# A four-layer gated cross-attention block: three transfers, a bias and half of the key pieces change engines

## What is computed

```python
x = x + tanh(g_xattn[0]) * L0_attention(layernorm(x), ctx)        # 16 heads of 16
x = x + tanh(g_ffn[0])   * L0_quantised_linear(layernorm(x))      # Hadamard, 4-bit levels, ternary weights
x = x + tanh(g_xattn[1]) * L1_attention(layernorm(x), ctx, mask)  # 16 heads, rotary positions
x = x + tanh(g_ffn[1])   * L1_top1_experts(layernorm(x))
x = x + tanh(g_xattn[2]) * L2_attention(layernorm(x), ctx, mask)  # 16 heads
x = x + tanh(g_ffn[2])   * L2_experts_with_capacity(layernorm(x))
x = x + tanh(g_xattn[3]) * L3_attention(layernorm(x), ctx)        # one head of 256
x = x + tanh(g_ffn[3])   * L3_top2_gated_experts(layernorm(x))
return x
```

```python
q, k, v = heads(x @ Wq + bq), heads(ctx @ Wk + bk), heads(ctx @ Wv + bv)   # 16 heads of 16
a = softmax(q @ k.T * scale, axis=-1)                                      # 512 x 1601 per head
out = concat(a @ v) @ Wo + bo
```

## Time and profile before

| | |
|---|---|
| median of 3 runs | 3863.64 us (3862.93 to 3868.33) |
| the profiled execution: its time | 3879.41 us |
| its span, first to last instruction | 3878.2 us |
| mean granted TensorE clock | 0.936 |
| busy share of the span: PE, DVE, ACT, POOL | 88%, 56%, 52%, 17% |

### The profile page before, as it was taken

The page is one execution under the profiler, slowest core; times in us unless marked ns, Lnnn a source line. Parts: engine busy times, 40 slices in busy tenths (PEclk is TensorE's granted clock), DMA queues, the critical chain, the costliest instruction groups (busy, mean ns, idle before and its releaser), DMA issues.

```text
span 3878.2 us, 52368 instructions
## 1 busy us (share of the span) xinstructions
PE 3417.0 (88%) x18396; PEld 1779.4 (46%) x18396; DVE 2178.5 (56%) x3567; ACT 2034.2 (52%) x4490; POOL 654.5 (17%) x700
## 2 busy tenths in 40 slices
PE   5899999978588899997899799889986979987997
PEld 2333333325332223332588333223325956677996
DVE  6767676736767677873401477768843032265333
ACT  2566666663236566766333267567671322244664
POOL 2111111001224331000302131210002110022331
PEclk8999999999789999999799799999997989998998
DMA  8132323106654443310965665754208521042555
GB/s 191 43 102 63 102 63 102 24 22 194 166 180 113 99 101 74 60 24 13 280 215 168 180 159 117 169 117 98 80 9 279 175 89 68 1 141 89 179 184 171
DMA packets 314686, 456.02 MB, mean 118 GB/s; under 512 B 66315, under 2 KB 234195, under 8 KB 312251
## 3 DMA queue, kind: packets, MB, share of 16 engines
q1 hardware_dynamic: 243382, 292.39, 28.0%
q0 software_dynamic: 29568, 104.65, 8.1%
q10 hardware_dynamic: 41477, 55.63, 5.5%
HBM read 292.46 MB, written 153.91 MB: 115 GB/s over the span
## 4 chain that ended last, share of the span: by engine, by line
PE 65%; DVE 13%; DMA 6%; issue 5%; POOL 4%; ACT 3%; SPq 2%; another core or an unknown queue 0%; ACTq 0%; POOLq 0%; DVEq 0%
PE pv L1334 14%; PE m L1298 10%; DVE mxp L1181 10%; PE s L1320 9%; PE h L2796 5%; PE y L2804 5%; PE h L2370 4%; PE y L2379 3%; PE y L1779 2%; PE s L1759 2%; PE s L1265 2%; PE m L1342 1%; ACT e_t L1412 1%; PE s L1282 1%; DMA ot<-sums 1%
## 5 line engine op out<-in xcount | busy, mean ns | idle before, releaser
L1181 DVE TENSOR_REDUCE mxp<-m 128x1 f32<-128x802 f32 x1536 | 1447.7, 985 | 523.0 <-PE m L1298 519.3
L1412 ACT ACTIVATE e_t<-s 128x512 f32<-128x512 f32 (+1 forms) x2496 | 1339.3, 599 | 575.7 <-PE s L1320 574.8
L1298 PE MATMUL m<-kaug,qaug 97*128 97x401 bf16 x3072 | 813.4, 347 | 115.9 <-DVE mxp L1181 66.3
L1320 PE MATMUL s<-qaug,kaug 100*128 100x512 bf16 (+1 forms) x2496 | 858.8, 387 | 22.6 <-ACT e_t L1412 18.3
L1334 PE MATMUL pv<-e_t,v 128*32 128x512 f32 (+1 forms) x4992 | 672.0, 611 | 0.2
L1320 PEld LDWEIGHTS s<-qaug,kaug 100*128 100x128 bf16 (+1 forms) x2496 | 228.5, 100 | 717.9 <-ACT e_t L1412 495.6
L1298 PEld LDWEIGHTS m<-kaug,qaug 97*128 97x128 bf16 x3072 | 274.1, 100 | 526.9 <-DVE mxp L1181 283.7
L127 POOL TENSOR_TENSOR rstd<-rstd,mhalf 128x16 f32<-128x16 f32 (+2 forms) x9 | 24.2, 2688 | 1207.3 <-DVE rstd L120 1207.3
L2866 ACT ACTIVATE ez<-h,b 128x128 f32<-128x128 f32 x440 | 120.1, 388 | 160.8 <-PE h L2796 160.8
L1334 PEld LDWEIGHTS pv<-e_t,v 128*32 128x32 f32 (+1 forms) x4992 | 98.7, 108 | 214.9 <-ACT e_t L1412 157.2
L2257 DVE SCALAR_TENSOR_TENSOR y<-y,b 128x256 f32<-128x256 f32 x39 | 16.5, 424 | 304.8 <-PE y L2379 304.8
(11 more groups left out here) (370 smaller groups left out, 3559.1 us busy)
## 6 DMA issues: line engine op xcount, KB each, us to landing
w<-in_L_w POOLq DMA_DIRECT2D x78, 1024.0 KB, 5.4
w<-in_L_w SPq DMA_DIRECT2D x24, 1024.0 KB, 12.3
xregion<-zero ACTq DMA_DIRECT2D x10, 2056.0 KB, 13.9
kaug<-kparts SPq DMA_DIRECT2D x16, 1200.8 KB
kaug<-kready SPq DMA_DIRECT2D x32, 600.4 KB
kaug<-kready SPq DMA_DIRECT2D x16, 1200.8 KB
vn<-values SPq DMA_DIRECT2D x8, 1536.0 KB
values<-p_vb ACTq DMA_DIRECT2D x21, 512.0 KB
```

Source lines behind the costliest of these rows:

```text
L1181: dve.tensor_reduce(a.mxp[:, u.g % 2, half, n:n + 1], a.m_slot[u.m % 2][:].rearrange("p (a n) -> p a n", a=2)[:, :, 0:PIECE + 1], AX.XY, A ...
L1298: m = pe.matmul(slot[:, 512 * k:512 * k + PIECE + 1], a.qaug[0:R_MAX, u.g, j, P * qc:P * qc + P], a.kaug[0:R_MAX, u.g, j, k0:k0 + PIECE + ...
L1320: pe.matmul(slot[0:KW[u.k], :], a.kaug[0:R_ALL, u.g, u.j, P * u.k:P * u.k + KW[u.k]], a.qaug[0:R_ALL, u.g, u.j, :], start=True, stop=True) ...
L1412: act.activation(a.e_t[0:KW[u.k], e % 2, u.j, :], a.s_slot[u.s % 3][0:KW[u.k], :], ACT.Exp).then_inc(s_free.sem, 1)
```

## The change

Three things are moved.

1. The store of the reciprocals and their spreading go from SP's queue to ACT's: "spread" is split into two units of the plan, "low" (store) and "spread" (read back), and ACT issues both. SP keeps `rc` and the four rows of `ot`. The semaphore `moved` keeps the four rows; `summed` counts the other three, and "rec" waits for the transfer to `rc` alone. With 6 steps (11 with outputs) the units stand at the scores 8, 15, 22, 30 and 44 ("sum", "rec", "low", "spread", "norm"), and with outputs at 8, 12, 16, 20 and 28, the outputs at 36, 40, 44 and 48.
2. The output bias is added by GpSimd, early in each attention (at the unit "bias"), to all of x in four instructions of 128 by 1024, and DVE's add behind each output (L1213) is left out.
3. The second of each chunk's two key pieces of the second attention is split by GpSimd, behind its steps of the quantised linear.

Three semaphores of the bias preparation become one (`b_made`), and `ident` gets another name; neither adds a wait. The diff, cut:

```diff
-NORM_STEPS = 5
-
-MOVES = 1 + HG + 2
+NORM_STEPS = 6
...
-        for kind in ("sum", "rec", "spread"):
+        for kind in ("sum", "rec", "low", "spread"):
             self.add(kind, b=b, g=g)
             yield
...
 def head_sum_sp(kn, a, u):
...
     if u.n:
-        sp.wait_ge(moved.sem, moved.at(MOVES * u.n))
+        sp.wait_ge(moved.sem, moved.at(HG * u.n))
+        sp.wait_ge(summed.sem, summed.at(3 * u.n))
...
-    sp.dma_start(a.rc[:], a.z[HD::P // HG, :]).then_inc(moved.sem, DMA)
+    sp.dma_start(a.rc[:], a.z[HD::P // HG, :]).then_inc(summed.sem, DMA)
     for j in range(HG):
         to, of = HG * HD * (u.g % 2) + HD * j, P // HG * j
         sp.dma_start(a.op[to:to + HD, u.g // 2, :], a.z[of:of + HD, :]).then_inc(moved.sem, DMA)
-def head_spread_sp(kn, a, u):
...
@@ head_pool
+        elif u.kind == "bias":
+
+            pool.wait_ge(b_made.sem, b_made.at(3))
+            for b in range(B):
+                xb = kn.x[:, TT * b:TT * b + TT, :]
+                pool.tensor_tensor(xb, xb, a.bob[:].rearrange("p (t n) -> p t n", t=1).to_broadcast([P, TT, D]),
+                                   ALU.add).then_inc(biased.sem, 1)
@@ head_dve
         elif u.kind == "rec":
-            dve.wait_ge(moved.sem, moved.at(MOVES * u.n + 1 + HG))
+            dve.wait_ge(summed.sem, summed.at(3 * u.n + 1))
             dve.reciprocal(a.rc[:], a.rc[:]).then_inc(r_full.sem, 1)
         elif u.kind == "norm":
-            dve.wait_ge(moved.sem, moved.at(MOVES * 2 * (u.n + 1)))
+            dve.wait_ge(moved.sem, moved.at(HG * 2 * (u.n + 1)))
+            dve.wait_ge(summed.sem, summed.at(3 * 2 * (u.n + 1)))
...
         elif u.kind == "out":
             xt = x[:, u.b * TT + u.k, :]
+            if u.k == 0:
+                dve.wait_ge(biased.sem, biased.at(u.b + 1))
             dve.wait_ge(m_full.sem, m_full.at(u.m + 1))
             dve.scalar_tensor_tensor(xt, a.m_slot[u.m % 2][:, 0:D], a.gate, xt, ALU.mult, ALU.add).then_inc(m_free.sem, 1)
-            dve.wait_ge(m_free.sem, m_free.at(u.m + 1))
-            i = dve.tensor_tensor(xt, xt, a.bob[:], ALU.add)
-    i.then_inc(x_done.sem, 1)
@@ head_act
+        elif u.kind == "low":
+            head_low_act(kn, a, u)
+        elif u.kind == "spread":
+            head_spread_act(kn, a, u)
         elif u.kind == "pv" and u.k == KT - 1:
             n = u.n // KT
             act.wait_ge(pv_done.sem, pv_done.at(u.n + 1))
             if n:
-                act.wait_ge(moved.sem, moved.at(MOVES * (n - 1) + 1 + HG))
+                act.wait_ge(moved.sem, moved.at(HG * n))
+                act.wait_ge(summed.sem, summed.at(3 * (n - 1) + 1))
             act.copy(a.z[:], a.pv[:]).then_inc(z_full.sem, 1)
+
+def head_low_act(kn, a, u):
+
+    act, r_full, summed = kn.nc.scalar, kn.sema("r_full"), kn.sema("summed", DMA)
+    sums = kn.dram["sums"]
+    act.wait_ge(r_full.sem, r_full.at(u.n + 1))
+    act.dma_start(sums.rearrange("j (a c) -> (j a) c", a=P // HG), a.rc[:]).then_inc(summed.sem, DMA)
+
+def head_spread_act(kn, a, u):
+    act, summed = kn.nc.scalar, kn.sema("summed", DMA)
+    act.wait_ge(summed.sem, summed.at(3 * u.n + 2))
+    lo = HG * HD * (u.g % 2)
+    act.dma_start(a.rs[lo:lo + HG * HD, u.g // 2, :],
+                 kn.dram["sums"].rearrange("j (a n) -> j a n", a=1).to_broadcast([HG, HD, T])).then_inc(summed.sem, DMA)
...
@@ the quantised linear
         a.p = Prepared(kn, sb, ahead, [s[:] for s in a.p_slot], (2, 0, 1), READY, rope,
-                       (*((1, ("dve",)) for _ in range(9)), (3, ("dve",))))
+                       (*((1, ("dve", "pool")) for _ in range(9)), (3, ("dve", "pool"))))
...
         pool.tensor_tensor(a.xq[:, u, :, :], q, h, ALU.add).then_inc(xq_made.sem, 1)
+        for part in ((), (3, 4), (5, 6), (7, 8))[i]:
+            prepare_split(kn, a.p, a.p.keys_of(part), pool, "pool")
+    prepare_split(kn, a.p, a.p.keys_of(9), pool, "pool")
     norm_pool(kn, "c")
```

More of the change, by code:

```diff
@@ L497, in add @@
             u.m = self.next("m")
-        if kind in ("pv", "turn", "sum", "rec", "spread", "norm", "take", "peak"):
+        if kind in ("pv", "turn", "sum", "rec", "low", "spread", "norm", "take", "peak"):
             u.n = self.next(kind)
@@ L778, in head_attention @@
             sig(name, DMA).close(n)
-        sig("moved", DMA).close(MOVES * NG * B)
-        ends = ["x_done", "s_free", "z_full", "r_full", "td", "moved"]
+        sig("moved", DMA).close(HG * NG * B)
+        sig("summed", DMA).close(3 * NG * B)
+        ends = ["m_free", "s_free", "z_full", "r_full", "td", "moved", "summed"]
         if not ready:
@@ L891, in head_sp @@
             head_sum_sp(kn, a, u)
-        elif u.kind == "spread":
-            head_spread_sp(kn, a, u)
         elif u.kind == "turn":
@@ L901, in head_sum_sp @@
 def head_sum_sp(kn, a, u):
-    sp, z_full, m_full, moved = kn.nc.sync, kn.sema("z_full"), kn.sema("m_full"), kn.sema("moved", DMA)
+    sp, z_full, m_full = kn.nc.sync, kn.sema("z_full"), kn.sema("m_full")
+    moved, summed = kn.sema("moved", DMA), kn.sema("summed", DMA)
     sp.wait_ge(z_full.sem, z_full.at(u.n + 1))
     if u.n:
-        sp.wait_ge(moved.sem, moved.at(MOVES * u.n))
+        sp.wait_ge(moved.sem, moved.at(HG * u.n))
+        sp.wait_ge(summed.sem, summed.at(3 * u.n))
     if u.b:
@@ L1134, in head_dve @@
     m_full, m_free, r_full, nm_full = (kn.sema(n) for n in ("m_full", "m_free", "r_full", "nm_full"))
-    ld, td, filled, b_scaled = kn.sema("ld", DMA), kn.sema("td", DMA), kn.sema("filled"), kn.sema("b_scaled")
-    bv_made, x_done = kn.sema("bv_made"), kn.sema("x_done")
+    ld, td, filled, b_made = kn.sema("ld", DMA), kn.sema("td", DMA), kn.sema("filled"), kn.sema("b_made")
     x, cst = kn.x, kn.cst
@@ L1139, in head_dve @@
     turns = units("turn")
-    ot_full, moved = kn.sema("ot_full"), kn.sema("moved", DMA)
+    ot_full, moved, summed, biased = kn.sema("ot_full"), kn.sema("moved", DMA), kn.sema("summed", DMA), kn.sema("biased")
     ld_q = kn.sema("ld_q", DMA)
@@ L1147, in head_dve @@
             i = dve.tensor_scalar(b_[:], b_[:], a.scale, None, ALU.mult)
-        i.then_inc(b_scaled.sem, 1)
+        i.then_inc(b_made.sem, 1)
     for u in plan.units:
@@ L1221, in head_pe @@
     ld_k, ld, rows, td = (kn.sema(n, DMA) for n in ("ld_k", "ld", "rows", "td"))
-    b_scaled, bv_made = kn.sema("b_scaled"), kn.sema("bv_made")
+    b_made = kn.sema("b_made")
     rope = a.rope is not None
@@ L1236, in head_pe @@
     if not a.ready:
-        ident = kn.sema("ident", DMA)
+        ident = kn.sema("tables", DMA)
         pe.wait_ge(ident.sem, ident.at(1))
@@ L1307, in head_pe @@
             slot = take_m(u.m)
-            pe.wait_ge(bv_made.sem, bv_made.at(1))
+            pe.wait_ge(b_made.sem, b_made.at(2))
             if not a.ready:
@@ L1348, in head_act @@
     s_full, s_free, m_free, pv_done = (kn.sema(n) for n in ("s_full", "s_free", "m_free", "pv_done"))
-    z_full, v_taken, b_scaled, filled = (kn.sema(n) for n in ("z_full", "v_taken", "b_scaled", "filled"))
+    z_full, v_taken, b_made, filled = (kn.sema(n) for n in ("z_full", "v_taken", "b_made", "filled"))
     ld_k = kn.sema("ld_k", DMA)
     rope = a.rope is not None
-    moved = kn.sema("moved", DMA)
+    moved, summed = kn.sema("moved", DMA), kn.sema("summed", DMA)
     if not a.ready:
@@ L2899, in first_loads_act @@
     act, w = kn.nc.scalar, a.w
-    ident, mask, gates = kn.sema("ident", DMA), kn.sema("mask", DMA), kn.sema("gates", DMA)
+    ident, mask, gates = kn.sema("tables", DMA), kn.sema("mask", DMA), kn.sema("gates", DMA)
     ld_q, rows, filled = kn.sema("ld_q", DMA), kn.sema("rows", DMA), kn.sema("filled")
@@ L2924, in setup_dve @@
     dve, cst = kn.nc.vector, kn.cst
-    ident, ready = kn.sema("ident", DMA), kn.sema("set")
+    ident, ready = kn.sema("tables", DMA), kn.sema("set")
     dve.memset(cst["ones"][:], 1.0)
@@ L2969, in setup_close @@
         kn.sema(name).close(1)
-    for name, n in (("const", 6), ("gates", 2), ("ident", 1), ("x_loaded0", 1), ("x_loaded1", 1), ("mask", 1), ("maskrow", 1)):
+    for name, n in (("const", 6), ("gates", 2), ("tables", 1), ("x_loaded0", 1), ("x_loaded1", 1), ("mask", 1), ("maskrow", 1)):
         kn.sema(name, DMA).close(n)
```

14 lines of the change are left out of this document (7 added, 7 removed).

## The result

The changed kernel took 3841.85 us (median of five runs, 3830.79 to 3847.38) against 3866.73 for the kernel before (3862.93 to 3868.33). The ratio is 0.9935, with a 95% interval of 0.9923 to 0.9948: faster by 25 us, 20 to 30 by the interval. The forecast was 3874 us, slower by 0.27%.

What follows compares the result with a forecast made beforehand. PE was taken to bound the attentions, DVE the linear stage between the first two. Terms -9 - 4.5 - 23 + 50 - 8 + 5 = +10.5 us gave 3874 us, slower by 0.27%; own range 3862 to 3888, all forecasts 3840 to 3905.

Steps and rivals of the forecast that it cites:

- Ends of the attentions (-9): At three attention tails, reciprocals start 2.5 us earlier and the last bias add goes: 2.9 us each, -9 us in all.
- Output bias (-4.5): Bias adds moved from DVE to GpSimd save 0.5 us for each of nine inner batches: -4.5 us.
- Second attention (-23): ScalarE issuing the reciprocals' transfers removes DVE's standing and the half clock behind it: -21 and -2, together -23 us.
- The -2 for the waits ahead of reciprocals: Second attention: a tenth of the 20 us that DVE stands ahead of reciprocals inside it is saved.
- Third attention, waits for the sums (+50): In eight ordinary groups the sums stand behind the clear in ScalarE's queue, stopping PE: 8 x 6.3, +50 us.
- landed 13.9 later: Third attention: the 2 MB clear lands 13.9 us after its issue, the median of the profile before.
- the half clock's 3.0: Third attention: 3.0 us more per group, lost to the half clock after PE's 3.3 us gap.
- The price of 6.3: Third attention: us per ordinary group, from PE's 3.3 us gap and 3.0 at the half clock behind it.
- The first rival: Third attention: the sums don't stand behind the clear, so the 50 falls away; -39.5, 3824 us, chance 0.17.
- the 16.9 us of the earlier trace: Third attention, group with outputs: SP could issue the spread only 16.9 us after a clear in another queue.
- Third attention, groups with outputs (-8): In three groups, an earlier spread shortens DVE's standing: -6.5, -2.4 and +1.2, together -8 us.
- Key pieces (+5): Linear stage: DVE and GpSimd take turns splitting pieces, +13, partly given back for GpSimd's work beside other operations: +5 us.

Runs made afterwards that it cites:

- spread sooner: The changed kernel, but in ordinary groups of the third attention ScalarE waits for the sums at the 26th score instead of the 30th; 3880.89 us, ratio 1.0035.
- sums by SP: The changed kernel, but in the third attention SP issues the sums' store, held back until ScalarE has finished the 22nd score; 3860.15 us, ratio 0.9980.
- the run with the spread later: The changed kernel, but in ordinary groups of the third attention ScalarE waits for the sums at the 39th score instead of the 30th; 3827.33 us, ratio 0.9898.

## Why the prediction was wrong

- **Ends of the attentions (-9): right.** The reciprocal starts 1.9 us after its transfer's issue instead of 4.4; PE's gap at the first end fell from 11.3 to 9.0 us. That makes about -7 for three.
- **Output bias (-4.5): too much credit, as far as is known.** By the profiles it is worth 0.3 us per group in the first attention, 0.9 for three groups; the 5.5 us between the medians are not settled. That these three groups won 4.5 us is the forecast's figure by luck: most of it is not the bias.
- **Second attention (-23): right in the main, and shown.** -20.8 in the profile, with the first group with outputs 17.8 shorter (forecast: 17); +17.7 with SP put back. The -2 for the waits ahead of reciprocals did not come: inside the attention they were 20.0 us and are 22.5, and the group behind the first outputs is 5.7 us longer than before, which the forecast did not have.
- **Third attention, waits for the sums (+50): this step failed, in its size.** That ScalarE would stand at the 30th score until the clear was through, that the sums would land right behind it (0.2 us; forecast 0.3), that PE would stop some 2 us later and go on one exponential after the spread, came as worked out. The term "landed 13.9 later" was wrong by 1.9 us: it was the median of the kernel before, and in the changed kernel it was 12.0. So PE's gap was at most 1.8 us and not 3.3, and the half clock's 3.0, which I had added to every one of them, did not follow: +12.3 instead of +50. The price of 6.3 was not far off for a gap with the half clock behind it: 6.5 us at gaps of 4.4 (spread sooner), 5.3 at 2.88 (sums by SP). I had 0 and 72 as bounds, and 45 to 60 in the forecast's own range.
- **In part the +12.3 is luck as well.** Five profiles have the clear, the sums and ScalarE's wait of these groups where the changed kernel has them. In three of them 6 of 24 such gaps were followed by the half clock; in the other two, the changed kernel's among them, none of 16 was. The changed kernel's profile is of its fastest execution, so 12.3 us is at the low end of what the waits cost; the run with the spread later gives 14.5 by the medians.
- **The reason given for it, the order in the queue, is not what makes the sums late**, without harm to the number: beside a clear they take as long in a queue of their own. The first rival's condition, sums within 10.2 us of the clear's issue, was missed by 1.5 to 2.5 us. What I held against that rival, the 16.9 us of the earlier trace rows, was misread: SP issued those sums only 8.6 us after the clear. In the ordinary groups of the kernel before they landed 10.0 to 11.3 us after the clear's issue, ahead of the clear itself.
- **Third attention, groups with outputs (-8): right**, -10.5 (63.6 to 55.5, 58.3 to 56.8, 43.9 to 42.9).
- **Key pieces (+5): not borne out, small.** Taking turns was right; that a pair would cost 11.6 us was not: 10.3. By the run with all pieces on VectorE the part gains 1.7 us, which can't be told from nothing.

With +12.3 in place of +50 alone, my own sum is -27, beside the measured -25. Why the clears landed sooner after the change than before is open. One difference is on record: before, SP's read-back of the sums and the stores held up behind it went out while the clear was under way (2341.88 and 2342.51, with the clear from 2331.43 to 2345.3); after, SP's last store ahead of the spread goes out at 2248.02, before the clear of 2253.66. No run tests it by itself.

## What to carry to other kernels

A small transfer whose landing an engine must wait for is better not issued while a large one is under way; another queue did not help here (9.5 us beside 9.2). Issuing the large one right behind the wait was worth 31 us here, more than the change itself. When a stall can bring a step with it (a clock that falls or doesn't), price it on both sides of the step: an error of 1.9 us in one transfer counted eight times here, and with it went a further 3.0 us a group that I had put down to the clock. And judge a move to another engine by what stands behind the wait on that engine: SP could wait 9.5 us for the sums at no cost, ScalarE not 3.

## What was not expected of the hardware

8 KB of sums took 9.2 us behind a 2 MB clear in one queue and 9.5 us beside it in another (twice, in the kernel before and with the sums by SP), where they took 1.4 us just ahead of one. By the Trainium skill ("DMA: Bandwidth & Descriptors", section "Queues, rings and completion order") a transfer engine goes round its queues packet by packet. The trace agrees in part: in the kernel before, sums in a queue of their own landed 2.4 to 4.3 us ahead of a clear that had been issued 1.0 us before them. But the wait is mostly ahead of the sums' first packet: in the eight groups it moved 4.5 to 6.1 us after the issue, in ScalarE's queue (q10) and in SP's (q1) alike, and 0.8 us after it where the clear came behind. Packets of the group of the earlier trace rows, before, all that the hardware queues moved from 2332.3 to 2337.5 us, and then SP's from 2337.5 to 2340 (packets, MB, share of 16 engines):

```profile
q10 hardware_dynamic: 1158, 1.19, 101.7%
...
q1 hardware_dynamic: 144, 0.01, 6.3%
```

The sums had been issued in q1 at 2332.39. Why their first packet waits no run shows.

The length of PE's gap alone did not tell whether the clock fell. With the spread sooner it fell towards 1.2 GHz behind all eight gaps, of 4.0 to 5.4 us. Among shorter ones it stayed at its upper level behind one of 2.27 us (all key pieces by VectorE) and fell behind one of 1.55 us (output bias by VectorE), in groups whose order is the same. PE and the window behind its gap, first the one run and then the other (PE, PEld, DVE, ACT, POOL, clock, DMA share, GB/s):

```profile
2271.93 0.88 PE L1311 MATMUL s<-qaug,kaug 100*128 100x512 bf16 x2 [2.27 <-ACT e_t L1403]
2271.93:2275.93 4.00, 3.64 (x23) 1.08 (x26) 1.87 (x6) 3.32 (x7) 0.00 (x0) 1.00 0.09 33
...
2314.14 1.09 PE L1305 MATMUL s<-qaug,kaug 100*128 100x512 bf16 x2 [1.55 <-ACT e_t L1397]
2314.17:2318.17 4.00, 4.00 (x15) 0.75 (x15) 1.87 (x6) 1.91 (x5) 0.00 (x0) 0.57 0.09 33
```
